# Three edge passes of a graph network on one core: sums counted by step in two PSUM halves, addresses worked out before the additions, float32 rows by rank

## The reference

```python
# layer 0, twice 64 + 32 + 32 inputs
all_feat = jnp.concatenate([x[dst], x[src], edge_attr, u_per_node[dst]], axis=-1)
msg = jax.nn.relu(all_feat @ W1 + b1)
agg = jax.ops.segment_sum(msg, dst, num_segments=x.shape[0])
x = relu(concatenate([x, agg, u_per_node]) @ W2 + b2)   # then residual, layer norm
# layers 1 and 2
h = x @ W + b
agg = jax.ops.segment_sum(h[src] + edge_attr @ We + be, dst, num_segments=N) + h
h = batchnorm(relu(agg) + bias)                          # the last: residual, layer norm
```

## Time and profile before

| what | us |
|---|---|
| median of 3 runs (16325.96 to 16482.94) | 16472.08 |
| the profiled execution's own time | 16175.08 |
| its span, first to last instruction | 16173.0 |
| POOL busy (3125 gathers in each of three passes, above all) | 9345.0 |
| PE busy (7128.5), PE weight loads | 4711.9 |
| DVE busy | 4849.1 |
| ACT busy | 409.6 |

### The profile page before, as it was taken

The page is one execution under the profiler, slowest core; times in us unless marked ns, Lnnn a source line. Parts: engine busy times, 40 slices in busy tenths (PEclk is TensorE's granted clock), DMA queues, the critical chain, the costliest instruction groups (busy, mean ns, idle before and its releaser), DMA issues. The chain is left out here.

```text
span 16173.0 us, 163998 instructions
## 1 busy us (share of the span) xinstructions
PE 7128.5 (44%) x32990; PEld 4711.9 (29%) x32990; DVE 4849.1 (30%) x13006; ACT 409.6 (3%) x818; POOL 9345.0 (58%) x9927
## 2 busy tenths in 40 slices
PE   4444445555455556444444444445334333333334
PEld 3333333333333334322222222223112111112112
DVE  2222223333233233322322222222322222223223
ACT  0000000000000000000000000000000000000000
POOL 5444444554555555566666666665666666666664
PEclk9665655555555555555555555555555555555555
DMA  2333333333333333111111111112111111111111
GB/s 69 70 67 67 67 69 73 72 72 73 71 72 73 72 72 69 36 34 34 34 33 34 34 34 34 34 34 43 30 23 23 23 23 23 23 23 23 23 23 32
DMA packets 1678800, 741.41 MB, mean 46 GB/s; under 512 B 1375715, under 2 KB 1518851, under 8 KB 1678608
## 3 DMA queue, kind: packets, MB, share of 16 engines
q1 hardware_dynamic: 1363054, 410.35, 11.9%
q0 software_dynamic: 315680, 330.31, 10.6%
HBM read 709.93 MB, written 29.75 MB: 46 GB/s over the span
## 5 line engine op out<-in xcount | busy, mean ns | idle before, releaser
L549 POOL DMA_INDIRECT rows<-source_table,index x6250 | 5899.3, 944 | 4677.1 <-issue 1998.3
L654 PE MATMUL sum_ps<-hit,message 128*64 128x128 f32 (+1 forms) x10000 | 2694.4, 429 | 3328.2 <-DVE by_rank L949 1606.8
L949 DVE TENSOR_TENSOR by_rank<-by_rank,sum_ps 64x128 f32 (+1 forms) x7500 | 2097.0, 280 | 6569.3 <-remote 3547.4
L549 POOL DMA_INDIRECT message<-source_table,index x3125 | 2947.9, 943 | 1687.7 <-issue 886.9
L654 PEld LDWEIGHTS sum_ps<-hit,message 128*64 128x64 f32 (+1 forms) x10000 | 1776.1, 227 | 4133.7 <-issue 1994.4
L654 PE MATMUL sum_ps<-hit,rows 128*64 128x128 f32 x5000 | 1440.8, 447 | 2430.3 <-DVE by_rank L949 1291.7
L937 DVE TENSOR_TENSOR hit<-out_ps,edge_place 128x640 f32<-128x640 f32 x1875 | 1538.1, 820 | 2049.8 <-issue 952.9
L654 PEld LDWEIGHTS sum_ps<-hit,rows 128*64 128x64 f32 x5000 | 721.4, 205 | 3149.3 <-DVE by_rank L949 1649.2
L628 PE MATMUL pre_ps<-w_edge,scratch 96*128 96x192 f32 x2500 | 957.3, 471 | 941.1 <-DVE summed_in L931 399.9
L632 PE MATMUL pre_ps<-scratch 128*128 128x64 bf16 x9375 | 759.0, 222 | 1222.1 <-issue 1221.2
L654 PE MATMUL stat_ps<-hit,message 128*64 128x128 f32 (+1 forms) x2500 | 813.3, 426 | 436.6 <-issue 251.8
(11 more groups left out here) (164 smaller groups left out, 1879.1 us busy)
## 6 DMA issues: line engine op xcount, KB each, us to landing
scratch<-ranked SPq DMA_DIRECT2D x3125, 48.0 KB
rows<-source_table,index POOLq DMA_INDIRECT x6250
scratch<-place_rows SPq DMA_DIRECT2D x625, 160.0 KB
scratch<-in_edge_t_steps SPq DMA_DIRECT2D x625, 96.0 KB
message<-in_edge_steps SPq DMA_DIRECT2D x625, 80.0 KB
message<-source_table,index POOLq DMA_INDIRECT x3125
xt<-in_x_t SPq DMA_DIRECT2D x28, 224.0 KB
index<-in_src_steps SPq DMA_DIRECT2D x375, 12.5 KB
```

Source lines behind the costliest of these rows:

```text
L549: nc.gpsimd.indirect_dma_start(to, None, source_table[l][:, :], bass.IndirectOffsetOnAxis(ap=index[:, at.j, s:s + 1], axis=0))\
L654: mm(tile_sum[s][0:w, :], (message if l < 2 else rows)[:, at.slot, s, 0:w], hit[:, at.half, s, :], start=True, stop=True).then_inc(tile_su ...
L949: V.tensor_tensor(at_rank, at_rank, tile_sum[s][0:w, :], ALU.add)\
```

## The change

1. **Sums counted by step.** `tile_sum(half, s)` puts a step's five sums into half of `sum_ps` (two banks), even and odd steps in turn. PE waits once a step, for the additions of the step two before, makes five matmuls, and counts `tile_summed` once. POOL, SP, ACT and DVE wait for the count of steps.
2. **Addresses ahead.** DVE computes the five addresses and the semaphore values of a step in three fused register instructions, waits once for the step's matmuls, and adds five times; the wait for the addition before is carried by the addition itself.
3. **Float32 rows by rank.** `ranked` holds one float32 row of 64 in place of three bfloat16 terms; `spread` is float32; each tile has one float32 matmul in place of three bfloat16 ones. The making of the terms becomes one copy on ACT.
4. **Byte offsets for SP.** A second table holds the ranks times 256; SP takes all five registers at once and addresses `ranked` by bytes. `eat` is counted on the window's semaphore, and a second wait for `pre_done` ahead of it is gone.

```diff
-PARTS = 3
-WIN = PARTS * F // 2
+ROW = F * 4
...
-        tile_sum = [sum_ps[:, s, 0:P] for s in range(4)] + [stat_ps[:, 0:P]]
+        def tile_sum(half, s):
+            return sum_ps[:, 2 * half + s // 4, s % 4 * P:(s % 4 + 1) * P]
...
-                        sp.reg_load(rank_regs, tile_ranks[:, bass.ds(m.number * S, S)])
+                        sp.reg_load(rank_regs, tile_bytes[:, bass.ds(m.number * S, S)])
+                        at_byte = [sp.snap(r, min_val=0, max_val=NPAD * ROW) for r in rank_regs]
                         for s in range(S):
-                            r = sp.snap(rank_regs[s], min_val=0, max_val=NPAD)
-                            sp.dma_start(window[:, m.slot, s, :], ranked[bass.ds(r, P), :])\
-                                .then_inc(window_in[m.slot], 16)
+                            sp.dma_start(window_bytes[:, m.slot, s, :], ranked_bytes[:, bass.ds(at_byte[s], P * ROW)]
+                                         .rearrange("o (p w) -> (o p) w", p=P)).then_inc(window_in[m.slot], 16)
...
-                        wait(sp, pre_done, m.number - RING + 1)
                         sp.dma_start(eat[:, m.slot, :, :],
...
-                        wait(pool, tile_summed[l], (at.number - RING + 1) * S)
+                        wait(pool, tile_summed[l], at.number - RING + 1)
...
                     for s in range(q, q + n):
-                        for c in range(PARTS):
-                            one = mm(pre_ps[:, m.half, s * F:(s + 1) * F], spread[:, m.half, s, :],
-                                     window_b[:, m.slot, s, c * F:(c + 1) * F], start=False,
-                                     stop=(c == PARTS - 1 and s == q + n - 1))
+                        one = mm(pre_ps[:, m.half, s * F:(s + 1) * F], spread[:, m.half, s, :], window[:, m.slot, s, :],
+                                 start=False, stop=(s == q + n - 1))
...
                     pe.wait_ge(hit_made[l], at.number + 1)
+                    wait(pe, tile_added[l], (at.number - 1) * S)
                     for s in range(S):
-                        wait(pe, tile_added[l], at.number * S + (s - 4))
-                        mm(tile_sum[s][0:w, :], (message if l < 2 else rows)[:, at.slot, s, 0:w],
-                           hit[:, at.half, s, :], start=True, stop=True).then_inc(tile_summed[l], 1)
+                        one = mm(tile_sum(at.half, s)[0:w, :], (message if l < 2 else rows)[:, at.slot, s, 0:w],
+                                 hit[:, at.half, s, :], start=True, stop=True)
+                    one.then_inc(tile_summed[l], 1)
...
                     if at.real:
                         for s in range(S):
-                            r = dve.snap(add_regs[s], min_val=0, max_val=NPAD)
-                            at_rank = by_rank[0:w, bass.ds(r, P)]
-                            dve.wait_ge(tile_summed[l], at.number * S + s + 1)
+                            dve.compute_val(at.number * S + s)
+                        at_rank = [by_rank[0:w, bass.ds(dve.snap(r, min_val=0, max_val=NPAD), P)] for r in add_regs]
+                        for to in at_rank:
+                            dve.lower_ap(to)
+                        dve.wait_ge(tile_summed[l], at.number + 1)
+                        for s in range(S):
...
-                            V.tensor_tensor(at_rank, at_rank, tile_sum[s][0:w, :], ALU.add)\
+                            V.tensor_tensor(at_rank[s], at_rank[s], tile_sum(at.half, s)[0:w, :], ALU.add)\
                                 .then_inc(tile_added[l], 1)
```

More of the change, by code:

```diff
@@ L127, in build @@
         eat = part(RING * 2 * P, STACK * C).rearrange("p (u n e) -> p u n e", u=RING, n=2)
-        window = part(RING * S * WIN).rearrange("p (u s w) -> p u s w", u=RING, s=S)
+        window = part(RING * S * F).rearrange("p (u s w) -> p u s w", u=RING, s=S)
+        window_bytes = window.bitcast(mybir.dt.uint8)
         place_row = part(RING * S * P // 2).bitcast(bf16).rearrange("p (u n) -> p u n", u=RING)
-        spread = part(S * P).bitcast(bf16).rearrange("p (u s e) -> p u s e", u=2, s=S)
+        spread = part(2 * S * P).rearrange("p (u s e) -> p u s e", u=2, s=S)
         assert at <= NB * F and NB * F + TILES <= SCRATCH
@@ L211, in build @@
         rows_in = [sem(f"rows_in_{u}") for u in slot]
-        eat_in = [sem(f"eat_in_{u}") for u in slot]
         ea_in = [sem(f"ea_in_{u}") for u in slot]
@@ L437, in steps @@
                     if at.real and m.real and m.slot == 0 and at.later:
-                        wait(sp, tile_summed[l], (m.number - CYCLE + RING) * S)
+                        wait(sp, tile_summed[l], m.number - CYCLE + RING)
                         load_index(m)
@@ L935, in steps @@
                     if m.real:
-                        wait(dve, tile_summed[l], (m.number - 1) * S)
+                        wait(dve, tile_summed[l], m.number - 1)
                         V.tensor_tensor(hit[:, m.half, :, :], over(along_ps, [P, S, P], 1),
```

64 lines of the change are left out of this document (27 added, 37 removed).

## The result

| | us |
|---|---|
| the kernel before, median on this chip (16312.23 to 16482.94) | 16399.02 |
| the changed kernel, median (15654.64 to 15693.79) | 15663.31 |
| ratio, 95% interval | 0.9555, 0.9488 to 0.9622 |
| the profiled execution's span | 15665.6 |

What follows compares the result with a forecast made beforehand. POOL's gathers (3900 us a pass) bound it, plus pauses for engines its run slows. 16175 - 500 (A) - 500 (B and C) - 10 (preparation) = 15165, times 1.018: 15440 us; range 14250 to 16450.

Steps and rivals of the forecast that it cites:

- the class that had 0.79: Whole kernel: faster by over 1%, below 16307 us; chance 0.79, of which the forecast itself 0.60.
- B and C, -500 us: Passes B and C: DVE's 13 instructions for 24 save 0.4 us a step, 250 us a pass.
- the balance of one cycle: B and C: POOL's run R, pause fixed at 3.5 us; R grows from 18.4 to 30 us, 6.95 us a step.
- rival 2: PE takes DVE's place as the late engine in B and C; time stays, 16300 to 16600 us; chance 0.12.
- Pass A, -500 us: Pass A: shorter pauses for DVE, less 0.5 us for lost catching up, give -0.8 us a step.
- Both at nothing: Pass A: SP's stall for the index and the smaller windows gain nothing; bound below, -0.5 us a step.
- 4.8 + 1.2 = 6.0: Pass A: float32 matmuls (+1.0) and spread (+0.2) lengthen a quick step to 6.0 us, just under POOL's 6.24.
- rival 3: Pass A: float32 matmuls and spread add 1.1 us a step, +690 us, making the kernel slower, 17170 us; chance 0.10.
- Preparation, -10: Preparation: ACT's and DVE's work on the terms goes, PE and POOL set the time; -10 us.
- PSUM halves at nothing: Sums of B and C: PE running ahead of DVE's additions through two PSUM halves costs nothing.
- The slow stretches: POOL's run slows the others to some 0.7 us an instruction on DVE; they fall behind, POOL pauses, all recovers.
- Rival 4: Slow stretches are loading of loop code; loops now fit, every pass falls to its floor, 13000 us; chance 0.03.

Runs made afterwards that it cites:

- e1: Changed kernel with PE leaving out two of five sums in B and DVE two of five additions in C; B 139 steps in 1000 us (4483 us), C 138 to 140.
- e3: Changed kernel without its third part: three bfloat16 terms and bfloat16 spread again; ratio to the kernel before 0.956.
- e8: Changed kernel with SP's window addresses as row offsets again, worked out ahead of each DMA; ratio to the kernel before 0.9843.
- e9: Kernel before with only SP's windows as byte offsets, all five worked out ahead of the DMAs; ratio to the kernel before 0.9828.
- e6: Changed kernel with the index loaded three steps earlier and POOL's first gathers in the preparation waiting for PE's groups; ratio to the kernel before 0.9557.
- e5: Changed kernel with sums counted and waited for tile by tile in B, addresses one by one in C; 15736.53 us beside 16319.04 for the kernel before.
- e2: Changed kernel with a memset that POOL waits for behind each step's gathers in B and C; B 139 steps in 1000 us, 7.2 us each.
- e7: Changed kernel with three gathers a step in B and seven in C instead of five; B 4.48 us a step, C 9.9 us.
- e11: Changed kernel with gathers of 64 rows instead of 128 in B; B 138 steps in 1000 us, 7.25 us a step.
- e12: Changed kernel with POOL's own break behind each step in all passes and first gathers paced by PE; ratio to the kernel before 0.924.

## Why the prediction was right, and where it wasn't

The sign and the range held, and the outcome is in the class that had 0.79. The size is seven tenths of the forecast, 4.5% for 6.3%. Of its two halves one failed, and the other came out by luck, from terms that were wrong each by itself.

- **"B and C, -500 us": failed.** Measured -85 between the two traces, -150 on one chip. The step that failed is the balance of one cycle: it kept "pauses 3.5" fixed while R grew, and took the others' speed in the stretch from DVE's 13 instructions. In the trace POOL's run grew from 15 to 20 gathers, not 25, and its pause with it, from 3.4 to 4.4 us. What came is near the lower bound ("nothing, if PE is late instead"): DVE waits for PE's count, as rival 2 had it; but e1 shows that the number of PE's records isn't the reason. A step of B and C takes 7.2 to 7.4 us with 20 or with 12 records for the sums, with 24 or 13 instructions on DVE, with stretches or without.
- **"Pass A, -500 us": the sum was right, its terms weren't.** Measured -468 between the two traces. That the sum is near is luck. I gave the gain to POOL's waits for DVE, which didn't fall (589 to 819 us over A), and charged the float32 matmuls 0.5 us. e3 shows the third part at nothing either way; e8 and e9 put about half of A's gain, 257 to 378 us, into SP's byte addresses, which I had at nothing.
- **"Both at nothing" (SP and index): failed.** e8 and e9 give SP's byte addresses 1.7 to 2.4%, 257 to 378 us, 0.4 to 0.6 us a step: the whole of the -0.5 that I had named as the bound. I had counted the instructions (17.5 to 13.5 a step) and trusted six steps of lead to cover them; what they cost in a slow stretch I never asked. Which side of the edit acts stays open.
- **The quick step of A, "4.8 + 1.2 = 6.0": right in size**, 6.21 us at the lower clock. But its term for the matmuls, "five take 2.13 us" against 1.15, sets a price from the earlier trace rows, where the granted clock was 1.00, beside one from the earlier trace rows, where it was 0.50. At 0.50 the five take 2.49 us, +1.3, and at 1.00 1.44. What the step was charged, +0.5 us, wasn't there: e3, without it, is no faster in A. The step stays just below POOL's 6.24, the point from which rival 3 decides.
- **`spread` "+0.2": right**, +0.16. By the Trainium skill's rule (VectorE: DVE Perf Modes, the perf-mode tier table) the estimate was +0.17; the trace agrees, 0.400 to 0.562 us.
- **"Preparation, -10": failed**, +55. The work on the terms that I took away was what made POOL pause; e3, with the terms back, starts its first gather at 336.2 us. It is the loop of cause that the prediction describes, in a place where I didn't look for it; pacing POOL gave 73 us back (e6).
- **PSUM halves at nothing: right** in B within 18 to 35 us (e5); in A it wasn't tried.
- **The slow stretches** themselves were read rightly: 0.7 us an instruction on DVE, a start some 10 us into POOL's run, an end after POOL stops. That the end comes 3 us after POOL was true only of runs of 15. What the prediction says of PE in a stretch, its records 0.7 to 1.0 us apart, holds in A and in the preparation; in B PE's rows of the changed kernel show nothing of the kind.
- Rival 4, the loading of loop code: nothing here speaks for it. The stretch in the preparation comes and goes with POOL's gathers.

What stays open is why a step of B and C costs 0.4 us and 1.36 us a gather, and what holds up PE's count of the sums in a stretch. That POOL's time and the others' are tied is shown by e2, e7 and e11; by what is not. With a break of 0.7 to 0.9 us POOL's own program is 7.0 to 7.2 us, so these runs can't tell whether a shorter break would bring a step below that; none was tried.

## What to carry to other kernels

Where one engine has to pause because the others are slow, and they are slow because of its own run, cheaper work for the others can lengthen the run and the pause alike; a short break written into the program of the engine that causes it, once a step, cost nothing in B and C, and in A, with the preparation's pacing, won 3.3% in all. A wait is credited to the engine it names only once it has been taken away: in A the wait for the index could be removed whole, and came back as a wait for DVE (e6). Where work is removed, ask which engine it had been holding back.

## What the runs showed of the hardware

- While POOL makes indirect DMAs one behind the other (0.94 us each, 0.30 between), after some 10 us in the passes (45 in the preparation, with four long gathers among them) DVE's instructions take 0.70 us each, and PE's matmuls in the preparation start 2.1 to 3.5 us apart, in multiples of 0.70. In the changed kernel's B the late thing is PE's count of the sums, of two steps at once. It goes on as long as POOL does (100 us in the preparation) and ends some 3 to 4 us after it stops in the cycles shown, 10.6 us after 98 gathers.
- A break of 0.92 us in every five gathers keeps this off altogether in B (all spacings of `hit` 6.3 to 8.1 us). With 0.71 us, in C of e2, POOL still pauses for the others, and with 0.73 us, in B of e12, 20 of 318 recorded counts come within 0.5 us of the one before.
- Gathers of 64 rows take 0.902 us, of 128 rows 0.947: the duration hardly goes with the rows.
